# One kernel, one change: x turned in 32x32 blocks by VectorE from batch 3 on, and w_lo of every other adapter unit made by GpSimd

## What is computed

```python
# layer 0: a dense layer and a signed one, both on x, added to x
output = jnp.einsum('bsi,oi->bso', x, W) + b
sign = (2 * mask - 1).astype(float32)                    # mask: 8 x 1024 x 1024 of int32
h = x + output + jnp.einsum('bsi,bio->bso', x, sign) * coeff[:, None, None]
# layer 1: one of 8 adapters per batch, picked by adapter_ids
out = h + jnp.einsum('bsi,boi->bso', h, weight[adapter_ids])
```

## Time and profile before

| | us |
|---|---|
| median of 3 runs | 399.57 (399.20 to 401.47) |
| the profiled execution | 400.16 |
| its span, first to last instruction | 398.4 |
| busy: PE / DVE / ACT / POOL | 389.9 / 356.3 / 256.9 / 51.6 |
| data read / written | 79.70 MB / 8.39 MB |

### The profile page before, as it was taken

One profiled execution on the slowest core, in us unless ns is written; L12 is line 12 of the kernel. 1 busy time (PEld: TensorE's weight loads), 2 busy tenths in 40 slices (PEclk: granted clock), 3 DMA queues, 4 the chain that ended last, 5 costly groups with the idle time before them and its releaser, 6 DMA issues.

```text
span 398.4 us, 7261 instructions
## 1 busy us (share of the span) xinstructions
PE 389.9 (98%) x2538; PEld 356.6 (90%) x2538; DVE 356.3 (89%) x349; ACT 256.9 (64%) x321; POOL 51.6 (13%) x78
## 2 busy tenths in 40 slices
PE   8898999999999999999999999999999999999996
PEld 8898999887899999999999999999999999999885
DVE  0699899989998899999999999999999999998830
ACT  2799776746666677676656685677666775765621
POOL 1022020111110101110020011001020101111200
PEclk9999999999999999999999999999999999999999
DMA  8999876997999999998988976999689995644511
GB/s 225 373 314 314 306 160 158 218 242 228 281 260 227 233 210 239 250 228 230 245 270 233 247 184 216 260 226 258 185 252 235 258 224 188 183 133 133 158 54 53
DMA packets 85031, 88.58 MB, mean 222 GB/s; under 512 B 28930, under 2 KB 69890, under 8 KB 84994
## 3 DMA queue, kind: packets, MB, share of 16 engines
q1 hardware_dynamic: 79152, 79.72, 78.3%
q10 hardware_dynamic: 5842, 8.40, 6.2%
HBM read 79.70 MB, written 8.39 MB: 221 GB/s over the span
## 4 chain that ended last, share of the span: by engine, by line
PE 77%; DVE 11%; ACT 5%; DMA 4%; issue 1%; SPq 1%; POOL 0%; DVEq 0%; POOLq 0%
PE second_ps L424 38%; PE first_ps L393 36%; DVE natural L699 2%; DVE w_lo_left L703 2%; ACT masks L495 2%; DMA natural<-in_L_cond_weight_dram 2%; DMA masks<-in_mask_Bx4096x_ik_dram 2%; PE turn_ps L376 2%; DVE masks L684 2%; ACT WT L490 1%; DVE M_lo L692 1%; DVE x_lo L709 1%; DVE h_lo L692 1%; DVE h_lo L720 1%; PE turn_ps L355 1%
## 5 line engine op out<-in xcount | busy, mean ns | idle before, releaser
L393 PE MATMUL first_ps<-x_lo,M_hi 128*128 128x256 f32 x416 | 118.4, 285 | 0.6 <-DVE M_lo L692 0.6
L393 PE MATMUL first_ps<-x_hi,M_lo 128*128 128x256 f32 x416 | 117.7, 283 | 0.0
L393 PE MATMUL first_ps<-x_hi,M_hi 128*128 128x256 f32 x416 | 117.7, 283 | 0.0
L510 ACT CAST M_hi<-masks 128x1024 fp32r<-128x1024 f32 (+1 forms) x57 | 57.6, 1010 | 76.3 <-DVE masks L684 55.6
L684 DVE SCALAR_TENSOR_TENSOR masks<-masks,coeffs,WT 128x1024 f32<-128x1024 f32 x60 | 77.9, 1304 | 13.6 <-ACT WT L490 13.6
L325 POOL TENSOR_TENSOR natural<-natural,ident 32x128 f32<-32x128 f32 x64 | 44.2, 690 | 291.5 <-DMA natural<-in_L_cond_weight_dram 291.5
L393 PEld LDWEIGHTS first_ps<-x_lo,M_hi 128*128 128x128 f32 x416 | 79.7, 192 | 1.9 <-DVE M_lo L692 0.8
L393 PEld LDWEIGHTS first_ps<-x_hi,M_hi 128*128 128x128 f32 x416 | 79.7, 192 | 0.9
L699 DVE STREAM_TRANSPOSE natural<-natural 128x1024 f32<-128x1024 f32 x64 | 78.8, 1234 | 1.6 <-POOL natural L325 1.6
L393 PEld LDWEIGHTS first_ps<-x_hi,M_lo 128*128 128x128 f32 x416 | 79.7, 192 | 0.0
L692 DVE TENSOR_TENSOR M_lo<-masks,M_hi 128x1024 fp32r<-128x1024 f32 (+1 forms) x57 | 67.0, 1175 | 3.5 <-ACT M_hi L510 3.5
(11 more groups left out here) (80 smaller groups left out, 542.1 us busy)
## 6 DMA issues: line engine op xcount, KB each, us to landing
natural<-in_L_cond_weight_dram SPq DMA_DIRECT2D x256, 128.0 KB, 3.8
masks<-in_mask_Bx4096x_ik_dram SPq DMA_DIRECT2D x60, 512.0 KB, 6.7
out_dram<-out_sb ACTq DMA_DIRECT2D x32, 256.0 KB, 4.1
x_nat<-in_x_dram SPq DMA_DIRECT2D x9, 512.0 KB, 7.1
W_nat<-in_L_cond_W_dram SPq DMA_DIRECT2D x8, 512.0 KB, 7.8
x_nat<-in_x_dram SPq DMA_DIRECT2D x80, 32.0 KB, 3.8
natural<-in_mask_Bx4096x_ik_dram SPq DMA_DIRECT2D x4, 512.0 KB, 8.1
natural<-in_x_dram SPq DMA_DIRECT2D x2, 512.0 KB, 9.4
```

Source lines behind the costliest of these rows:

```text
L393: done = nc.tensor.matmul(acc(b, u), left, right, start=(k == 0 and u % 2 == 0 and j == 0), stop=(k == K - 1 and u % 2 == 1 and j == 2))
L510: done = nc.scalar.copy(part.rearrange("p u (a j) -> p a u j", j=SQ), whole[:, :, u0:u0 + part.shape[1], :])
```

## The change

Two things are changed together.

**x half 0.** From batch 3 on half 0 is handled as half 1 was: `load_x_blocks(b, half, k)` replaces the whole load. SP issues the sets for half 0 at i = 0, 1, 2 and once more at i = 2, four transfers each; DVE turns them at i = 4 (`turn_x_blocks(b + 1, 0)`); PE's `turn_x(b + 1, 0)` at i = 4 is gone, and x_hi, x_lo of half 0 read the turned blocks in SBUF and not turn_ps. ACT's `round_x(b, 0)` now waits for the turned blocks and for the first four steps of the batch before.

**w_lo.** `is_pooled(g)` holds for even g from 12 on: 26 units. Their subtraction leaves DVE and is issued by POOL behind `add_diagonal(g + 1)`; it waits for w_hi of its unit. `wait_w` splits the old count w_done in two, w_done (DVE's) and w_pooled (POOL's), for SP's loads and PE's `second`. Odd units stay with DVE.

```diff
...
@@ -154,6 +155,22 @@
         def M_lo_place(b, k):
             return M_place(b, k, M_lo, h_lo, w_lo_right)
+        def is_pooled(g):
+            return g >= 12 and g % 2 == 0
+        def pooled_before(g):
+            return sum(map(is_pooled, range(g)))
+        def wait_w(engine, g):
+            engine.wait_ge(w_done, g + 1 - pooled_before(g + 1))
+            if pooled_before(g + 1):
+                engine.wait_ge(w_pooled, pooled_before(g + 1))
+        def subtract_w_hi(engine, g):
+            return engine.tensor_tensor(w_part(w_lo, g), turned_unit(g), w_part(w_hi, g).bitcast(F32), ALU.subtract)
         def turned_unit(g):
             return natural[:, g % RING, :].rearrange("p (c u r) -> p u c r", c=GRP, r=SQ)
...
@@ -231,7 +245,7 @@
                     sp.wait_ge(M_done, 9 + g)
                 if g >= RING:
-                    sp.wait_ge(w_done, g - RING + 1)
+                    wait_w(sp, g - RING)
                 who = sp.value_load(ids_row[0:1, g // K:g // K + 1], min_val=0, max_val=weight.shape[0] - 1)
                 m = g % K
                 for a in range(GRP):
@@ -239,16 +253,15 @@
                                  weight[bass.ds(who, 1), m * P:(m + 1) * P, a * Q:(a + 1) * Q]
                                  .rearrange("a (c r) f -> r (a c) f", r=SQ)).then_inc(natural_loaded[g % RING], DMA)
-            def load_x_blocks(b, k):
-                if b == BLOCK_X:
-                    sp.wait_ge(x_turned, turned_count(b - 1, 1) + 1)
-                else:
-                    sp.wait_ge(x_done, half_count(b - 1, 1) + 1)
+            def load_x_blocks(b, half, k):
+                sp.wait_ge(x_turned if b == BLOCK_X else x_done, half_count(b - 1, half) + 1)
                 for q in range(GRP):
-                    at = HALF + k * P + q * SQ
-                    sp.dma_start(x_blocks[q * SQ:(q + 1) * SQ, k * S:(k + 1) * S].rearrange("r (g j) -> r g j", j=SQ),
-                                 x[b, :, at:at + SQ].rearrange("(g r) j -> r g j", r=SQ)).then_inc(x_loaded[1], DMA)
+                    at = half * HALF + k * P + q * SQ
+                    sp.dma_start(x_blocks(half)[q * SQ:(q + 1) * SQ, k * S:(k + 1) * S]
+                                 .rearrange("r (g j) -> r g j", j=SQ),
+                                 x[b, :, at:at + SQ].rearrange("(g r) j -> r g j", r=SQ)
+                                 ).then_inc(x_loaded[half], DMA)
             load_x(0, 0)
             load_W(0)
@@ -305,10 +318,13 @@
                     load_mask(n + RING)
                 if n - 2 < CHUNKS:
                     load_unit(n - 2)
-                if 3 <= i < 7 and b + 1 < B:
-                    load_x_blocks(b + 1, i - 3)
-                if i == 2 and b + 1 < B:
-                    load_x(b + 1, 0)
+                if b + 1 < B:
+                    if i < 3:
+                        load_x_blocks(b + 1, 0, i)
+                    if i == 2:
+                        load_x_blocks(b + 1, 0, 3)
+                    if 3 <= i < 7:
+                        load_x_blocks(b + 1, 1, i - 3)
             for t in range(2):
                 sp.wait_ge(stored[t], DMA * 2 * B)
@@ -337,7 +353,13 @@
             for g in range(CHUNKS):
                 if g:
                     pool.wait_ge(w_diag_added, g)
+                if pooled_before(g - 1):
+                    pool.wait_ge(w_pooled, pooled_before(g - 1))
                 add_diagonal(g)
+                if is_pooled(g - 1):
+                    pool.wait_ge(w_diag_added, g + 1)
+                    pool.wait_ge(w_hi_done, g)
+                    subtract_w_hi(nc.gpsimd, g - 1).then_inc(w_pooled, 1)
         @block.tensor
         def _(pe):
@@ -362,9 +384,7 @@
                 else:
                     pe.wait_ge(x_loaded[half], DMA * max(b, 1))
                 n = half_count(b, half)
-                if b > BLOCK_X:
-                    pe.wait_ge(x_done, half_count(b - 1, 0) + 1)
-                elif b < 2:
+                if b < 2:
                     pe.wait_ge(WT_done, W_BEFORE_X[n])
                 elif n == 4:
@@ -413,7 +433,7 @@
                 if t == 0:
                     pe.wait_ge(h_done, K * (b + 1))
                 if t % ST == 0:
-                    pe.wait_ge(w_done, K * b + 4 * q + 4)
+                    wait_w(pe, K * b + 4 * q + 3)
                 if b or t >= 2:
                     pe.wait_ge(out_taken, 4 * b + t - 1)
                 for u in range(K):
@@ -476,8 +496,6 @@
             for n in range(OPEN, CHUNKS):
                 b, i = n // K, n % K
                 first(n)
-                if i == 4 and b + 1 < B:
-                    turn_x(b + 1, 0)
                 if i % 2:
                     second(b - 1, i // 2)
             for t in range(4):
@@ -526,12 +544,12 @@
             def round_x(b, half):
                 source = turned_x
-                if b >= BLOCK_X and half:
-                    act.wait_ge(first_done, K * b)
-                    act.wait_ge(x_blocks_turned, b - BLOCK_X + 1)
-                    source = x_blocks.rearrange("p (k s) -> p k s", s=S)
+                if b >= BLOCK_X:
+                    act.wait_ge(first_done, K * b - (1 - half) * K // 2)
+                    act.wait_ge(x_blocks_turned, 2 * (b - BLOCK_X) + half + 1)
+                    source = x_blocks(half).rearrange("p (k s) -> p k s", s=S)
                 else:
-                    act.wait_ge(x_turned, turned_count(b, half) + 1)
+                    act.wait_ge(x_turned, half_count(b, half) + 1)
                 nc.scalar.copy(x_half(x_hi, h_hi, b, half), source).then_inc(x_hi_done, 1)
             def round_h(b):
@@ -700,18 +718,17 @@
             def rest_w(g):
                 dve.wait_ge(w_hi_done, g + 1)
-                nc.vector.tensor_tensor(w_part(w_lo, g), turned_unit(g), w_part(w_hi, g).bitcast(F32), ALU.subtract
-                                        ).then_inc(w_done, 1)
+                subtract_w_hi(nc.vector, g).then_inc(w_done, 1)
             def rest_x(b, half):
-                source = x_blocks.rearrange("p (k s) -> p k s", s=S) if b >= BLOCK_X and half else turned_x
+                source = x_blocks(half).rearrange("p (k s) -> p k s", s=S) if b >= BLOCK_X else turned_x
                 dve.wait_ge(x_hi_done, half_count(b, half) + 1)
                 nc.vector.tensor_tensor(x_half(x_lo, h_lo, b, half), source,
                                         x_half(x_hi, h_hi, b, half).bitcast(F32), ALU.subtract).then_inc(x_done, 1)
-            def turn_x_blocks(b):
-                dve.wait_ge(x_loaded[1], DMA * (2 + K // 2 * GRP * (b - BLOCK_X + 1)))
-                nc.vector.transpose(x_blocks, x_blocks).then_inc(x_blocks_turned, 1)
+            def turn_x_blocks(b, half):
+                dve.wait_ge(x_loaded[half], DMA * (2 + K // 2 * GRP * (b - BLOCK_X + 1)))
+                nc.vector.transpose(x_blocks(half), x_blocks(half)).then_inc(x_blocks_turned, 1)
             def rest_h(b):
                 for u in range(K):
@@ -797,14 +814,17 @@
                     rest_M(n + 1)
                 if n == CHUNKS - 1:
                     turn_w(g + 1)
-                rest_w(g)
+                if not is_pooled(g):
+                    rest_w(g)
                 if b >= BLOCK_X and i == 1:
-                    turn_x_blocks(b)
+                    turn_x_blocks(b, 1)
+                if i == 4 and b + 1 < B:
+                    turn_x_blocks(b + 1, 0)
                 if b >= BLOCK_X and i == 2:
                     rest_x(b, 1)
                 if i == 6 and b + 1 < B:
                     rest_x(b + 1, 0)
-                if n == CHUNKS - 1:
+                if n == CHUNKS - 1 and not is_pooled(g + 1):
                     rest_w(g + 1)
                 if i == 7:
                     if n + 2 < CHUNKS:
@@ -812,7 +832,7 @@
                     rest_h(b)
             for g in range(CHUNKS - 4, CHUNKS):
                 turn_w(g)
-                if g > CHUNKS - 4:
+                if g > CHUNKS - 4 and not is_pooled(g - 1):
                     rest_w(g - 1)
             rest_w(CHUNKS - 1)
```

More of the change, by code:

```diff
@@ L109, in build @@
         w_done = sem("w_done")
+        w_pooled = sem("w_pooled")
         x_turned = sem("x_turned")
@@ L171, in x_arrives, with x_blocks @@
             return natural[:, :ST, half * HALF:(half + 1) * HALF] if b == 1 else x_nat[:, half, :, :]
-        x_blocks = x_nat[:, 1, :, :].rearrange("p s c -> p (s c)")
+        def x_blocks(half):
+            return x_nat[:, half, :, :].rearrange("p s c -> p (s c)")
         def x_part(tile, h, b):
@@ L183, in half_count @@
             return 2 * half + b if b < 2 else 2 * b + half
-        def turned_count(b, half):
-            return half_count(b, half) if b < BLOCK_X else 2 * BLOCK_X + b - BLOCK_X
         turned_x = turn_ps[:, :, :].rearrange("p n (k s) -> p (n k) s", s=S)
@@ L219, in load_x @@
                 if b >= 2:
-                    sp.wait_ge(x_turned, turned_count(b - 1, half) + 1 if b > 2 else 3)
```

(1 more changed line is left out.)

## The result

The changed kernel takes 420.71 us (median of 5 runs, 420.23 to 421.40), the kernel before 399.57: a ratio of 1.052, 95% interval 1.049 to 1.055. The prediction was 415.5 in a range of 398 to 430, slower with 0.77. The profiled execution took 421.29 us, with a span of 419.5.

The account below looks back on a forecast made before the run. PE bounds the old kernel, DVE right behind; after the change DVE was to bind at 49.3 us per batch. Profiled 400.16 + 15.9 = 416.1, less 0.59 to the median: 415.5 us, range 398 to 430.

Parts of the forecast that it names:

- PE: -4.35 us: PE loses five groups of x half 0 transposes of 0.87 us each, batches 3 to 7; new period 44.87 us.
- PE's waits for h_lo and M_lo: Sign of a right forecast: in the loop PE waits for DVE's M_lo and h_lo, 3 to 4 us per batch.
- DVE's work of 40.8 us per batch: DVE's 44.2 us net per batch, less four rest_w (4.6), plus one more transpose of x blocks (1.16).
- The exclusion, 2.15 us per subtraction: GpSimd's moved subtraction keeps out DVE operations with two SBUF operands for 2.15 us; waits of 8.0 us per batch.
- The cycle: DVE's period per batch: 40.8 work + 8.0 waits + 0.5 stretches = 49.3 us, against the old 45.74.
- The start: Batch 2, first moved units: M of step 25 ready at 150.5 us with stretches; PE 2 us late there.
- The end: Units 60 and 62 on GpSimd, diagonals 62 and 63 queued behind 60: taken as 0, at most 2.3 us.
- Loads and queues at nothing: SP's 15 extra transfers (+6.8 us per batch), delayed loads and GpSimd's queue order: costed at nothing.
- No exclusion: Rival: GpSimd's long operation is interleaved with DVE's or holds under 1.1 us; PE stays the bound, 395.2 us; chance 0.14.
- A shorter holding: Rival: holding 1.1 to 1.5 us, or GpSimd late enough to run beside turn_w; 397.6 to 402 us; chance 0.09.
- A GpSimd slowed by strided views: Rival: strided views of natural and w_lo cost more; holding 2.8 to 3.6 us, 428 to 444 us; chance 0.08.
- SP or the x blocks: Rival: no exclusion, but DVE waits for x_loaded; 395.2 + 13 = 408 us; chance 0.03.

Follow-up runs that it names:

- the reordered kernel: Changed kernel, complete, with the next sign ahead of w_hi in i = 1, 3, 5, 7 and DVE's x-block turns behind add_sum of steps 2 and 6: 395.26 us.

## Why the prediction was right

**PE: -4.35 us.** Right as far as it goes: no turn_ps work in the loop, and the reordered kernel gets just this. "This is worth its full price only while DVE needs no more than 44.87" decided the case, and the run with the x half alone shows it: 403.85 and not 395.2. PE's waits for h_lo and M_lo, forecast as 3 to 4 us per batch, are 11.4 + 4.6 = 16.0 us, or 3.2 for each of the five batch ends.

**DVE's work of 40.8 us per batch.** The batch from add_sum at 202.42 to add_sum at 252.23 has 49.81 us. Less the four waits (8.19), the wait for x_hi (0.56) and two stretches by diagonals (0.24 and 0.13) it is 40.7. Right.

**The exclusion, 2.15 us per subtraction.** Eight times the stretch of 0.25 us seen beside a 128-element operation is 2.0, and the prediction took 2.15 between that and its upper bound of 2.8; measured 2.2. That the holding grows in proportion to the length was assumed there and shown only by the run with half the length; that the value chosen between the bounds came within 0.05 was in part luck, and the prediction itself named it as its least certain step. Its other estimate, 2.25 us in all and 2.05 of holding, was too low: 2.40 and 2.2. The waits add up to 8.19 us per batch, forecast 8.0. Its place was right too: GpSimd comes in 0.15 us behind w_hi, and add_sum can't be first because its sign is behind w_hi. The run with the sign first shows that this order made the difference between 420.7 and 397.3 us. The prediction named that as part of a rival ("late enough to run beside turn_w after an add_sum") and priced it at about 400; it gave 397.3.

**What was too small, 5.2 us in all (421.29 against 416.1).** Three terms:
- The cycle, 49.8 in place of 49.3, four times: 2.0 us. The waits for GpSimd were 0.2 more than forecast, and the 0.89 us of DVE's idle time in the old batch were all taken as slack. Some 0.6 of them were DVE waiting for x_hi, which ACT makes behind w_hi and the sign of the same step; they stay in the new batch (0.56). Idle time is only slack if what ends it comes earlier when the engine is late.
- The start: M_lo of step 25 ends at 151.47, forecast 150.5: 1.0 us. The loop began 0.5 us later in this execution, and the same wait for x_hi (0.67) is in batch 2 too.
- The end, taken at 0 with a bound of 2.3: 1.9 us from step 57 on (that step is 19.2 us late, the end 21.1). The run that leaves the last three units on DVE gets 2.2 us back. The mechanism written down was the right one, the value taken the wrong one.

These are 4.9 us against the +16.2 of step 57. The other 0.3 is the prediction's own last step, from +16.2 down to +15.9. All three terms erred to the same side.

**Loads and queues at nothing.** Right: DVE never waits for x_loaded in the trace of the changed kernel, and the block loads land after 3.3 us at the median, 6.6 at most. SP waits 23 us in all for GpSimd's subtractions, but behind 56 us neither ACT nor DVE waits for a load.

**The rivals.** No exclusion: refuted by the 2.63 us of add_sum. A shorter holding: 2.2 us. A GpSimd slowed by strided views: 2.40 us, in all cases within 0.03. SP or the x blocks: no wait of DVE for x_loaded, and 414.4 us without the new block loads.

## What to carry to other kernels

Before work is moved to an idle engine, look in the trace for the shortest existing operation of the same kind there and at what happened to its neighbours: a stretch of 0.25 us beside 128 elements was the price of the whole change. Where two engines exclude each other, the moment counts for more than the amount: put the long operation beside those that don't take part (here DVE's transposes and operations with a PSUM operand) and look at what the waiting engine could do instead, and what makes that late. And a gain on the engine that bounds is only as large as the lead of the second engine. That lead is less than its idle time: DVE idled 0.9 us per batch, and 0.6 of it stayed when DVE got more work.

## What the runs showed of the hardware

- GpSimd: 2.40 us for a subtraction of 128x1024 of float32, 1.30 for 128x512, 1.04 for a copy of 128x1024, 0.95 for a fill. Reading, one operand or two, excludes DVE's operations with two SBUF operands; filling doesn't.
- What I had not expected is PE's clock. PE waited 2.27 us for h_lo and began again at 246.61; the granted clock of the stretch from 246 to 250 was 0.64, where the one before it has 1.00, which is a fall from 2.4 to 1.2 GHz for most of the stretch. 48 matmuls took 7.66 us in place of 5.75:

```profile
242.00:246.00 4.00, 2.35 (x11) 1.61 (x9) 3.11 (x4) 4.00 (x11) 3.67 (x2) 1.00 1.07 209
246.00:250.00 4.00, 3.39 (x18) 3.42 (x19) 4.00 (x10) 1.34 (x3) 0.45 (x1) 0.64 0.82 187
250.00:254.00 4.00, 4.00 (x32) 3.88 (x32) 3.99 (x4) 2.47 (x3) 0.00 (x0) 0.94 0.60 203
```

(Length, then busy us and count of PE, PEld, DVE, ACT and POOL, the granted clock, the DMA share, GB/s.) A wait of this size doesn't always have this effect. In the loop of this execution PE waited five times for h_lo before a first product. The clock fell behind three of these waits (1.97, 2.27 and 2.39 us, PE back at 147.01, 246.61 and 346.19) and stayed at 1.00 behind the other two (2.39 and 2.37 us, back at 196.81 and 296.40). What decides it was not tested. Here a fall costs nothing more, since DVE sets the length of the batch: batches with and without it are both 49.8 us. In a kernel that PE bounds a wait with such a fall would cost about 1.9 us more than itself (an estimate, 7.66 - 5.75; no run here shows it).
